# Three of eight gathers of transposed key pages issued by ScalarE's queue, and keys read by columns eight steps earlier

## The reference

```
q = x @ Wq.T ; k = x @ Wk.T ; v = x @ Wv.T       # 32 query heads, 8 key heads, head size 128
q, k = rope(rmsnorm(q)), rope(rmsnorm(k))
kc = k_cache[block_table].reshape(bsz, 512, 8, 128)   # 16 pages of 32 keys for each sequence
vc = v_cache[block_table].reshape(bsz, 512, 8, 128)
probs = softmax(where(valid, q @ concat(kc, k).T * SCALE, -1e30))     # 640 keys
x = x + (probs @ concat(vc, v)) @ Wo.T
```

## Time and profile before

| | us |
|---|---|
| median of 3 runs | 1445.12 (1442.46 to 1446.32) |
| the profiled execution, its own time | 1446.37 |
| its span in the profile | 1444.6 |
| TensorE busy | 1393.5 |
| DVE, ACT, POOL busy | 1100.4, 843.5, 808.4 |

### The profile page before, as it was taken

How to read it: one execution, slowest core, us unless ns; L and a number is a source line. 1 busy time by engine, 2 the same in 40 slices (tenths; PEclk the granted TensorE clock), 3 DMA queues, 4 the chain that set the end, 5 groups by cost and what they waited for, 6 DMA issues and landing times.

```text
span 1444.6 us, 26952 instructions
## 1 busy us (share of the span) xinstructions
PE 1393.5 (96%) x8004; PEld 1210.6 (84%) x8004; DVE 1100.4 (76%) x2209; ACT 843.5 (58%) x2072; POOL 808.4 (56%) x801
## 2 busy tenths in 40 slices
PE   2899999999999999999999999999999999899999
PEld 1788888888888888888888888888888788688887
DVE  4788888888888888888888888888888566554544
ACT  1566666666666666666666667676676322433332
POOL 5555555555555666666666666666566320454342
PEclk9899999999999999999999999999999999999999
DMA  4433343333333322232322222222323440233441
GB/s 127 138 103 110 114 117 101 101 103 103 103 101 104 95 71 66 65 76 68 70 64 65 65 69 76 66 67 47 116 59 94 114 96 22 91 120 120 121 120 67
DMA packets 192705, 129.87 MB, mean 90 GB/s; under 512 B 119088, under 2 KB 159792, under 8 KB 190256
## 3 DMA queue, kind: packets, MB, share of 16 engines
q1 hardware_dynamic: 192560, 128.15, 32.1%
HBM read 125.24 MB, written 24.64 MB: 104 GB/s over the span
## 4 chain that ended last, share of the span: by engine, by line
PE 81%; SPq 12%; issue 3%; DVE 1%; DMA 1%; POOL 1%; ACT 1%; DVEq 0%
PE banks L311 19%; PE banks L312 19%; PE banks L313 19%; PE banks L1275 10%; PE banks L1252 8%; SPq L357 6%; SPq L341 3%; SPq L365 2%; PE banks L1216 2%; DMA w_raw<-in_w_att 1%; PE banks L1490 1%; PE banks L1504 1%; PE banks L1317 1%; PE banks L1443 1%; SPq L336 1%
## 5 line engine op out<-in xcount | busy, mean ns | idle before, releaser
L695 ACT ACTIVATE prob<-prob,nbias 128x640 f32<-128x640 f32 x256 | 210.4, 822 | 148.6 <-DVE nbias L908 148.6
L883 DVE TENSOR_TENSOR pt_pair<-banks,pt_pair 128x640 fp32r<-128x640 f32 x256 | 211.0, 824 | 108.3 <-ACT pt_pair L691 105.7
L908 DVE CUSTOM_DVE_ANT_0 prob<-banks,mask,q_rs 128x640 f32<-128x640 f32 x256 | 220.3, 879 | 42.8 <-PE banks L313 42.6
L1275 PE MATMUL banks<-w_pair,o_pair 128*128 128x512 f32 x768 | 224.1, 414 | 0.0
L691 ACT ACTIVATE pt_pair<-banks 128x640 fp32r<-128x640 f32 x256 | 179.3, 700 | 44.1 <-PE banks L1252 44.1
L311 PE MATMUL banks<-w_pair,x_pair 128*128 128x256 f32 (+1 forms) x512 | 179.1, 350 | 20.9 <-POOL w_pair L489 20.9
L1252 PE MATMUL banks<-ident,prob 128*128 128x128 f32 x1280 | 185.3, 276 | 3.5 <-DVE pt_pair L883 3.5
L1252 PEld LDWEIGHTS banks<-ident,prob 128*128 128x128 f32 x1280 | 147.4, 140 | 45.2 <-issue 33.2
L312 PE MATMUL banks<-w_pair,x_pair 128*128 128x256 f32 (+1 forms) x512 | 174.0, 340 | 0.0
L313 PE MATMUL banks<-w_pair,x_pair 128*128 128x256 f32 (+1 forms) x512 | 173.3, 339 | 0.0
L311 PE MATMUL banks<-kt_pair,qt_pair 128*128 128x320 f32 x512 | 164.9, 322 | 2.2 <-DVE kt_pair L883 2.2
(11 more groups left out here) (176 smaller groups left out, 3433.4 us busy)
## 6 DMA issues: line engine op xcount, KB each, us to landing
w_raw<-in_w_att SPq DMA_DIRECT2D x64, 320.0 KB, 3.2
w_raw<-in_fw SPq DMA_DIRECT2D x66, 256.0 KB, 3.3
x_raw<-in_xT SPq DMA_DIRECT2D x64, 256.0 KB, 3.2
kt_all<-in_kT SPq DMA_DIRECT2D x128, 128.0 KB, 2.5
kv_raw<-in_kv SPq DMA_DIRECT2D x416, 32.0 KB, 1.6
kt_raw<-kt_all SPq DMA_DIRECT2D x38, 256.0 KB, 3.0
kv_raw<-in_kv SPq DMA_DIRECT2D x608, 16.0 KB, 1.5
fb_all<-in_gu_b SPq DMA_DIRECT2D x32, 176.0 KB
```

The lines of the kernel that those rows point to most:

```text
L695: act.activation(prob[:, h, :], prob[:, h, :], ACT.Exp, bias=nbias[:, h:h + 1], scale=-1.0, accum_out=psum_row[:, h:h + 1]).then_inc(exped, 1)
L883: dve.tensor_tensor(pair[1], src, pair[0].bitcast(F32), ALU.subtract).then_inc(lo_sem, 1)
L908: dve.tensor_tensor_reduce(out=prob[:, h, :].rearrange("p (a n) -> p a n", a=2), in0=score_ps[h % 2][:, :, 0:HALF], in1=mask[:, n % B, :]. ...
L1275: last = pe.matmul(misc_ps, o_pair[:, j, h, :], w_pair[:, k, ds(at + h * HID, HID)], start=i == 0, stop=i == 3 * REP - 1)
```

## The change

`BY_ROWS` falls from 26 to 18, so the gathers go with the loads of steps 2 to 17: eight for each of these 16 steps, of which SP issues the first five and ACT the last three. ACT issues its three at the end of its step n (n = 0 to 15, for step n + 2), behind `pt_high(n, 2)` and ahead of `exponent(n + 1, 0)`; ahead of them it reads three page numbers from DRAM itself.

```diff
-BY_ROWS = 3 * B + 2
+BY_ROWS = 2 * B + 2
+ACT_GATHERS = 3
...
+        def gathers(n):
+
+            part = (n - 2) // B
+            return range(part * NPP // 2, (part + 1) * NPP // 2)
+
+        def gather_page(e, b, j, page):
+
+            e.dma_start(kt_all[b, j].rearrange("g d s -> g (d s)"),
+                        t["kT"][ds(page), :, :].rearrange("a g n -> (a g) n")).then_inc(s_gathered[(b - 2) % B // HB], 16)
...
                 if 2 <= n < BY_ROWS:
-                    gather_keys(b, pages, (n - 2) // B)
-
-            def gather_keys(b, pages, part):
-
-                for j in range((part * NPP + 2) // 3, (part * NPP + NPP + 2) // 3):
-                    sp.dma_start(kt_all[b, j].rearrange("g d s -> g (d s)"),
-                                 t["kT"][ds(pages[j]), :, :].rearrange("a g n -> (a g) n")).then_inc(s_gathered[(b - 2) % B // HB], 16)
+                    for j in gathers(n)[:-ACT_GATHERS]:
+                        gather_page(sp, b, j, pages[j])
...
                 pt_high(n, 2)
+                if n + 2 < BY_ROWS:
+                    b, some = (n + 2) % B, gathers(n + 2)[-ACT_GATHERS:]
+                    _, pages = nc.values_load_multi_w_load_instructions(
+                        t["pages"][ds(b), some.start:some.stop], engines=[act.engine], min_val=0, max_val=PAGES - 1,
+                        skip_runtime_bounds_check_because="page numbers are below PAGES")
+                    for j, page in zip(some, pages):
+                        gather_page(act, b, j, page)
```

## The result

| | median, us | runs |
|---|---|---|
| before | 1445.72 | 4 (1442.46 to 1447.65) |
| after | 1458.32 | 4 (1454.07 to 1461.24) |

A forecast was written before the change was run, and what follows sets the result against it. SP's issue was taken to bound about the first eleven steps, TensorE all others. -3.1 - 3.8 + 0.5 = -6.4 us on 1446.37 us gave 1440.0 us, 1439 us as median; own range 1436 to 1442 us, 8 in 10: 1436 to 1455 us.

The forecast's parts named there:

- ACT's block: Two register loads and three gathers behind `pt_high(n, 2)`, 16 times: 3.5 to 4.0 us each, +0.5 us in total.
- free lateness: ACT's next exponential may start 0.8 us late before DVE delays TensorE; anything beyond lengthens the step by as much.
- SP's relief: One gather fewer on SP in steps 2 to 9, 0.67 us each; 3.8 us of the early loss comes back.
- The third term: Steps 18 to 25 go by columns and lose four transposes each: 8 x 0.39 = 3.1 us less.
- overlap: At the step's end ACT's queue starts the pointer load while the copy runs; lateness 0.6 us, or 1.1 us if dear.
- The load of three numbers: ACT's register load of page numbers: 0.37 us from a line through eight and 16 numbers, 0.87 us at the other end.
- early loss: First eleven steps take 192.96 us instead of 188.65 us; these 4.3 us were put down to SP's issue.
- rival C: ACT's register loads cost what they cost on SP behind transfers: +9 to +18 us, 1454 to 1463 us; chance 0.18.
- Rival B: ACT's queue reads the pointer only after the copy ends: -1 to +7 us, about 1448 us; chance 0.20.
- Rival D: The early loss comes of SP's transfers, not their issue, so nothing comes back: -2.6 us, 1442.5 us; chance 0.10.

The follow-up runs named there:

- The ladder: Kernel before the change, with register loads of 1 to 16 numbers added behind ACT's last work, each kept by a small DMA; three numbers took 1.23 us.
- the load of eight numbers: Changed kernel, but ACT reads all eight page numbers of the half row and uses the last three: 1452.05 us.
- the runs with three, four, five and none on ACT: Changed kernel with ACT issuing three, four or five of eight gathers in pieces, SP the rest: 1448.38, 1443.28, 1440.11 us; SP issuing all eight: 1461.85 us.
- fixed pages: Changed kernel without ACT's register loads; its three gathers a step take page numbers fixed when the program is built: 1441.65 us.

## Why the prediction was wrong

Two terms of the sum failed. ACT's block, put at +0.5 us, cost 18.7 us, for its load of page numbers was priced too low and the free lateness too high; and SP's relief, put at -3.8 us, is not there even in the version in which ACT costs nothing. The third term, -3.1 us, held.

**Keys by columns from step 18: right.** Steps take 16.77 us eight steps sooner, 8 x 0.39 = 3.1 us. The gathers were ready.

**The block's place and its overlap: right.** ACT's queue begins with the pointer while the copy runs, in all 16 blocks; in the one shown the copy starts at 294.83, and the pointer load of 1.03 us ends at 295.87. The pointer took 0.87 us at the median (0.93 in the mean), with 0.82 us predicted, and the gathers 0.52 us at the median, 0.66 us apart, with 0.49 and 0.67 us predicted. Rival B (no overlap) is out.

**The load of three numbers: the term that failed most.** I took 0.37 us from a line through 8 and 16 numbers, with 0.87 us as the other end. It takes 1.26 to 1.51 us, 1.29 at the median, outside both. The ladder and the load of eight numbers show the cause: three numbers are three pieces, eight are two. The bound was taken as if a smaller load could not cost more than a larger one. This is 0.9 us in each of 16 blocks, nearly 15 us.

**What DVE lets pass: too generous.** The prediction's argument amounts to a step of 13.4 us plus the time from the start of the copy to the exponential (2.99 us and 0.8 us of slack make 17.15 us). Measured are 13.69 us in the later steps, as in the one at 294.83. Two things make the difference. The 0.2 us between the end of `pt_low` and TensorE's transpose were no slack: 0.14 to 0.15 us lie between the two in both kernels, also where TensorE waits for just this. And DVE's stretch from the third `mask_min` on takes 0.2 us longer, since its product of queries and cosines takes 1.13 us in the steps with a block and 0.83 us in the others; why, no run shows. The free lateness was thus 0.5 us (17.15 - 13.69 - 2.99) and not 0.8 us. In steps 1 to 6, which hold a mask, 14.08 us stand in place of the 13.69 us.

**A gather now and then is dear.** Of the 48 gathers in the 16 blocks five hold ACT for 0.95 to 1.31 us, and one pointer load takes 1.44 us. From the start of the copy to the exponential pass 4.3 to 5.4 us, 4.63 us in the mean of the 16. With 16 x (13.69 + 4.63) = 293.1 us and 6 x 0.39 = 2.3 us for the masks the sum meets the measured 295.4 us. The block alone is 16 x (13.69 + 4.63 - 17.15) = 18.7 us, where the sum had 0.5 us.

**One gather fewer on SP, -3.8 us: did not come.** The early loss has two parts, which I had put down to SP's issue alone. The masks are about 0.3 us in each of six steps; the run without them shows it. The rest is SP, as the runs with three, four, five and none on ACT show, but five gathers on SP with three on ACT are no relief: the 16 steps with fixed pages, where ACT costs nothing, take 281.4 us, in the kernel before 279.7 us. Two readings failed here. I took one round of 17.1 us without a dear issue for SP's round with six gathers; the mean of the eight is 17.56 to 17.80 us. And I took 0.67 us off it for the gather that ACT issues, where less than 0.3 us came off (17.52 us), and SP's load of page numbers got 0.3 us longer. With three gathers on SP the steps from the seventh on are at 17.15 us. That SP's issues get longer behind ACT's gathers is shown by their place in time throughout the stretch, and by its absence where ACT issues nothing; what the two share is not shown.

**The rivals.** The measured 1458.3 us lies in rival C's range of 1454 to 1463 us, in which the register loads cost as much on ACT as they do on SP behind transfers. The size and the direction were those of C, but the mechanism was not: the pointer was cheap, and the load of the numbers cost 1.3 us for a reason of its own, so that the time fell in C's range is partly luck. Rival D gave 1442.5 us, near the run with fixed pages, where ACT costs nothing and the early loss stays; but its mechanism, the transfers, is out, since the same transfers issued otherwise run in 278.1 us. I had given C 0.18, since I had let the cheap end of an unknown price decide.

## What to carry to other kernels

Work put in the gap of an engine that runs in order is free up to the gap and what the next engine can absorb, and costs its full excess each time beyond; the same work in pieces, each in a gap of its own, can be free for that engine, as ACT's three gathers here. What is left then is the first queue's: +12.6 us with one block became +3.4 us with three gathers in pieces, and -4.8 us with five. Bound the price of an operation that the trace does not show by an operation of the same shape, not by a line through larger ones: smaller is not always cheaper. And moving the issue of transfers from one queue to another relieves the first only by what the second does not cost it back; count rounds of the first queue after the move, not instructions.

## What the runs showed of the hardware

A register load on ACT costs about 0.4 us a piece: 1, 2, 3 numbers 0.47, 0.83, 1.23 us; four from a place that is a multiple of four 0.48 us, four from place 1 1.61 us; eight 0.91 us, sixteen 1.81 us (on SP 1.67 us and more). The pointer load ahead of it takes 0.86 to 0.87 us at the median (1.04 us in one version) and up to 1.6 us now and then, and it runs beside a copy: in the changed kernel it starts within 0.01 us of the copy's start, 16 times of 16. A gather issued by ACT holds its queue for about 0.5 us (0.61 us at the median with page numbers fixed in the program), and the copies in flight go on meanwhile: in the version with three gathers in pieces one is issued from 226.79 to 227.29 while a copy runs from 226.66 to 227.37. Page loads on SP that end 1.2 to 2.3 us behind the start of such a gather often take 0.4 to 0.9 us in place of 0.32 us, in the version with three in pieces. Single DMA issues of 1.0 us and more occur on SP in all versions; on ACT single gathers took 0.9 to 1.7 us in six versions, and none over 0.64 us in the two with three and four gathers in pieces.
